# Two stacked cross-attention layers: the work between the two attention loops, done per pair of batches inside the first loop

## The reference

```python
# layer 0: 16 heads of 8
qkv = x @ w_qkv + b_qkv
x = layer_norm(x + mha(q, k, v) @ w_so + b_so, ln_g, ln_b)
ca = mha(x @ w_q + b_q, y @ w_k + b_k, y @ w_v + b_v) @ w_co + b_co
x = layer_norm(x + ca, ln_g, ln_b)
h = relu(relu(x @ w1 + b1) @ w2 + b2)          # 128 -> 512 -> 512
x = layer_norm(x + h @ w3 + b3, ln_g, ln_b)
# layer 1: 16 heads of 64
h = layer_norm(x, gamma, beta)
attn = softmax((h @ Wq) . (context @ Wk)) * 64 ** -0.5
x = x + (attn . (context @ Wv)) @ Wo + bo
```

## Time and profile before

| what | us |
|---|---|
| median of 3 runs | 1124.32 (1124.01 to 1125.93) |
| the profiled execution's own time | 1120.81 |
| its span, first to last instruction | 1119.0 |
| PE busy | 1036.5 (93%) |
| PE loading weights | 737.2 (66%) |
| DVE busy | 756.5 (68%) |
| ACT busy | 570.2 (51%) |
| POOL busy | 390.0 (35%) |
| mean granted clock of PE | 0.960 |

### The profile page before, as it was taken

How to read it: one execution, slowest core, us unless ns; L and a number is a source line. 1 busy time by engine, 2 the same in 40 slices (tenths; PEclk the granted TensorE clock), 3 DMA queues, 4 the chain that set the end, 5 groups by cost and what they waited for, 6 DMA issues and landing times. The chain is left out here.

```text
span 1119.0 us, 31601 instructions
## 1 busy us (share of the span) xinstructions
PE 1036.5 (93%) x12044; PEld 737.2 (66%) x12044; DVE 756.5 (68%) x1406; ACT 570.2 (51%) x1135; POOL 390.0 (35%) x273
## 2 busy tenths in 40 slices
PE   5975899999999998979697999999999999999997
PEld 2551576666666665655534777777777777777786
DVE  4646778887788878520685676767767677767652
ACT  2531577776777765742244444444444444444442
POOL 4823111111211123020103554555545455545542
PEclk9886899999999999989798999999999999999998
DMA  3503533444434443030002111111111111111100
GB/s 98 140 2 104 145 118 124 132 138 143 132 121 124 148 141 89 2 98 1 1 23 72 46 48 56 39 37 56 53 56 50 38 53 31 45 53 56 35 3 4
DMA packets 47021, 79.90 MB, mean 71 GB/s; under 512 B 6978, under 2 KB 33812, under 8 KB 46964
## 3 DMA queue, kind: packets, MB, share of 16 engines
q1 hardware_dynamic: 46964, 79.10, 23.6%
HBM read 50.93 MB, written 21.96 MB: 65 GB/s over the span
## 5 line engine op out<-in xcount | busy, mean ns | idle before, releaser
L1362 ACT ACTIVATE P<-PS 125x448 f32<-125x448 f32 x384 | 207.1, 544 | 270.0 <-PE PS L1271 268.0
L1252 POOL TENSOR_TENSOR Pl<-P 125x896 f16<-125x896 f32 x128 | 229.9, 1801 | 241.9 <-ACT P L1362 241.9
L1000 DVE TENSOR_REDUCE m<-PS 128x1 f32<-128x500 f32 x336 | 220.7, 674 | 119.8 <-PE PS L991 118.0
L906 DVE TENSOR_REDUCE m_part<-PS 128x1 f32<-128x500 f32 x336 | 212.4, 674 | 64.1 <-PE PS L809 62.9
L884 ACT ACTIVATE Pb<-PS 125x448 f32<-125x448 f32 x384 | 187.9, 544 | 36.2 <-PE PS L784 34.8
L1287 PE MATMUL PS<-cNh,P 125*128 125x97 f16 x1344 | 197.9, 208 | 0.1
L1289 PE MATMUL PS<-cNh,Pl 125*128 125x97 f16 x1344 | 197.4, 207 | 0.0
L1288 PE MATMUL PS<-cNl,P 125*128 125x96 f16 x1344 | 196.8, 206 | 0.0
L1288 PEld LDWEIGHTS PS<-cNl,P 125*128 125x128 bf16 x1344 | 131.8, 98 | 25.4
L1287 PEld LDWEIGHTS PS<-cNh,P 125*128 125x128 bf16 x1344 | 131.2, 98 | 15.8 <-issue 3.2
L809 PE MATMUL PS<-KH,Qmx 128*128 128x500 f16 x336 | 129.6, 388 | 11.9 <-PEq L682 8.2
(11 more groups left out here) (167 smaller groups left out, 1531.2 us busy)
## 6 DMA issues: line engine op xcount, KB each, us to landing
Kst<-k_halves SPq DMA_DIRECT2D x144, 125.0 KB, 2.7
k_halves<-KH SPq DMA_DIRECT2D x16, 750.0 KB, 3.3
cx<-in_ctx SPq DMA_DIRECT2D x16, 562.5 KB
d_cx<-in_ctx SPq DMA_DIRECT2D x16, 562.5 KB
c_halves<-cHi SPq DMA_DIRECT2D x16, 281.2 KB, 2.6
c_halves<-cLo SPq DMA_DIRECT2D x16, 281.2 KB, 3.2
cTh<-c_halves SPq DMA_DIRECT2D x16, 281.2 KB, 3.0
cTl<-c_halves SPq DMA_DIRECT2D x16, 281.2 KB, 3.9
```

Source lines behind the costliest of these rows:

```text
L906: nc.vector.tensor_reduce(m_part[:, t, part:part + 1], PS[:, 6 + k % 2, 0:SP], AX.X, ALU.max).then_inc(s_reduced, 1)
L1000: nc.vector.tensor_reduce(m21[:, t, part:part + 1], PS[:, S1[k % 2], 0:SP], AX.X, ALU.max).then_inc(n_red, 1)
L1252: nc.gpsimd.tensor_tensor(Pl[:, c % NP], P1[:, c % NP], high, ALU.subtract).then_inc(n_low_p, 1)
L1362: nc.scalar.activation(P1[:, c % NP, half * HALF:(half + 1) * HALF], PS[0:KC, u % 3, 0:HALF], ACT.Exp).then_inc(n_exp, 1)
```

## The change

The stage in the middle is left only for the last pair of batches. For the pairs t = 0 to 6 its work is done within the loop of the first cross attention, in the bodies of the pair after it (`mid`, t = i - 1), in matmuls of 112 columns into one bank, FB = 2, which the scores give up (SBANKS is 2 where they had 3). The square root is worked out on DVE by three Newton steps. The weights' transposes and products go to the opening, beside the maximum pieces of batch 0; the tile Wvo now lies in Pb's memory. The absorbed queries go to DRAM (`qk_halves`) and are loaded from there. Cut to its core:

```diff
+        def absorb(pe, t, r):
+            if r == 0: pe.wait_ge(f_kept, t * 2 + 2)
+            elif r == 1: pe.wait_ge(att_kept, ...)
+            else: pe.wait_ge(g_low, t * 4 + r - 1)
+            for k in range(4):
+                mm = pe.matmul(PS[0:DC, G_BANKS[r], k * TP:(k + 1) * TP], Wqk[:, 4 * r + k, :], Tm[:], start=True, stop=True)
+        def spread_of(dve, at, src):
+            dve.wait_ge(f_link, at)
+            nc.vector.bn_stats(st6[:], src).then_inc(f_link, 1)
+            dve.wait_ge(f_link, at + 1)
+            nc.vector.memset(passed[:], 0.0)
+            nc.vector.bn_aggr(mv[:], st6[:]).then_inc(f_link, 1)
+            dve.wait_ge(f_link, at + 2)
+            nc.vector.tensor_scalar(half_var[:], mv[:, 1:2], EPS, -0.5, ALU.add, ALU.mult).then_inc(f_link, 1)
+            dve.wait_ge(f_link, at + 3)
+            nc.vector.tensor_scalar(root[:].bitcast(I32), half_var[:].bitcast(I32), -0.5, ROOT_GUESS, ALU.mult, ALU.add).then_inc(f_link, 1)
+            for n in range(ROOT_STEPS):
+                dve.wait_ge(f_link, at + 4 + 2 * n)
+                nc.vector.tensor_scalar(grown[:], root[:], root[:, 0:1], half_var[:, 0:1], ALU.mult, ALU.mult).then_inc(f_link, 1)
+                dve.wait_ge(f_link, at + 5 + 2 * n)
+                nc.vector.tensor_scalar(root[:], grown[:], 1.5, root[:, 0:1], ALU.add, ALU.mult).then_inc(f_link, 1)
+            dve.wait_ge(f_link, at + SPREAD)
+        def norm_cross(dve, t):      # add, spread_of, normalise into nm
+        def norm_hidden(dve, t):     # add, spread_of, gain and bias into Xm
+        def norm_twice(dve, t):      # spread_of(Xm), normalise into nm
...
 first cross attention, SP
+                    if par == 1 and not (isinstance(i, int) and i < 1):
+                        store_queries(sp, i - 1)       # waits g_low t * 4 + 4, two DMAs
 POOL
                         wait_for(pool, st_done, b * NC * 2)
+                        wait_for(pool, m_laid, b + 1)
...
+                    if isinstance(i, int) and b == 0:
+                        norm_to_residual(pool, x_steps, R_CO)
+                    if isinstance(i, int) and b == -1:
+                        pool.wait_ge(wvo_kept, 4)
+                        nc.gpsimd.tensor_tensor(Wvo16[:, 1], Wvo, Wvo16[:, 0], ALU.subtract).then_inc(wvo_split, 1)
+                    if par == 1 and not (isinstance(i, int) and i < 1):
+                        residual(pool, i - 1)
+                        move_residual(pool, i - 1)
 PE
                 turn_context, k == 0:
+                if par == 0 and mode == LOOP:
+                    wait_for(pe, g_low, (i - 1) * 4)
                 scores_t:
+                        if isinstance(i, int) and n == 0:
+                            pe.wait_ge(wvo_kept, 4)
-                        wait_for(pe, exp_done, n * 2 * NC + u - 2)
+                        wait_for(pe, exp_done, n * 2 * NC + u - 1)
                 body, step c:
+                        if mid and par == 1 and c < 4:
+                            hidden_2(pe, t, c)         # before the step's second piece
                         for k in pieces[1:]:
                             score_piece(i, par, k)
+                        if at_start and c < 3:
+                            turn_weights(pe, c)
+                        if at_start and c in (6, 9):
+                            multiply_weights(pe, (c - 6) // 3)
+                        if mid and par == 0:           # c == 9: out_project, 12: turn_pair(0), 13: hidden_1
+                        if mid and par == 1:           # c == 5: hidden_3, 9: turn_pair(1), c >= 10: absorb(c - 10)
 ACT
+                    if isinstance(i, int) and b == 0:
+                        act.wait_ge(wvo_split, 1)
+                        # even: c == 12 keep_pair(0), 13 keep_hidden(0)
+                        # odd: c == 4 keep_hidden(1), 9 keep_pair(1), c >= 10 queries_high(c - 10)
 DVE
+                        if mid and par == 1:
+                            if c == 6:
+                                norm_hidden(dve, t)
+                            if c == 8:
+                                norm_twice(dve, t)
                         for k in pieces[1:]:
                             reduce_piece(i, par, k)
...
                         nc.vector.tensor_tensor(mneg[:, QT:], mhigh[:], mtop[:], ALU.subtract).then_inc(m_ready, 1)
+                        if mid and par == 0:
+                            norm_cross(dve, t)
+                        if mid and par == 1:
+                            queries_low(dve, t, 0)
                         dve.wait_ge(m_turned, n + 1)
...
+                    if mid and par == 1:
+                        for r in range(1, 4):
+                            queries_low(dve, t, r)
 stage in the middle
-                (all of it)
+                SP: load_halves of batch 0, d_cx, load_halves of batch 1, store_queries(NT - 1)
+                PE, ACT, DVE, POOL: the same steps for t = NT - 1, one after the other,
+                PE: out_project, pieces 0-3, turn_pair(0), piece 4, hidden_1, pieces 5-7, hidden_2,
+                    pieces 8-9, hidden_3, pieces 10-16, turn_pair(1), piece 17, absorb(0..3) with pieces 18-20
+                DVE: norm_cross, reductions 0-9, norm_hidden, norm_twice, reductions 10-17, queries_low(0..3) with 18-20
```

More of the change, by code:

```diff
@@ L89, in spread, with over_pairs @@
     return ap.unsqueeze(dim).broadcast_to(shape[:dim] + [n] + shape[dim:])
-def over_pairs(eng, body, before=(), last=1):
+def over_pairs(eng, body, before=(), last=1, first=1):
     for i, par in before:
         body(i, par)
-    for par in (0, 1):
-        body(0, par)
-    with eng.Fori(1, NT - last) as i:
+    for i in range(first):
+        body(i, 0)
+        body(i, 1)
+    with eng.Fori(first, NT - last) as i:
         body(i, 0)
@@ new lines, in hidden_2, with hidden_3 @@
+        def hidden_2(pe, t, m):
+            if m == 0:
+                pe.wait_ge(f1_kept, t + 1)
+            for k in range(4):
+                mm = pe.matmul(PS[:, FB, m * TP:(m + 1) * TP], w2s[:, k, m * 128:(m + 1) * 128], hid1[:, k, :], start=(k == 0), stop=(k == 3))
+            if m == 3:
+                mm.then_inc(f2, 1)
+        def hidden_3(pe, t):
+            pe.wait_ge(f2_kept, t + 1)
+            for k in range(4):
+                mm = pe.matmul(PS[0:TP, FB, 0:D], hid2[:, k, :], w3s[:, k, :], start=(k == 0), stop=(k == 3))
+            mm.then_inc(f3, 1)
@@ new lines, in move_residual, with store_queries @@
+        def move_residual(pool, t):
+            pool.wait_ge(f_normed, t * 2 + 2)
+            pool.wait_ge(table_in, 16)
+            nc.gpsimd.tensor_copy(X[:, bass.ds(t, 1), :], Xm[:].unsqueeze(1)).then_inc(x_moved, 1)
+        def store_queries(sp, t):
+            sp.wait_ge(g_low, t * 4 + 4)
+            for half in range(2):
+                sp.dma_start(qk_halves[bass.ds(t * 2, 2), half].rearrange("b p n -> p b n"),
+                             QKs[:, half].rearrange("p j h q -> p j (h q)")).then_inc(qk_out, 16)
@@ new lines, in pieces @@
+                def pieces(at, n):
+                    for k in range(at, at + n):
+                        score_piece1(pe, -1, 1, k)
+                out_project(pe, t)
+                pieces(0, 4)
+                turn_pair(pe, t, 0)
+                pieces(4, 1)
+                hidden_1(pe, t)
+                pieces(5, 3)
+                for m in range(4):
+                    hidden_2(pe, t, m)
+                pieces(8, 2)
+                hidden_3(pe, t)
+                pieces(10, 7)
@@ L1179, in program, with pieces @@
-        ffn.close()
+                t = NT - 1
+                def pieces(at, n):
+                    for k in range(at, at + n):
+                        reduce_piece1(dve, -1, 1, k)
+                norm_cross(dve, t)
+                pieces(0, 10)
+                norm_hidden(dve, t)
+                norm_twice(dve, t)
+                pieces(10, 8)
+                for r in range(4):
+                    queries_low(dve, t, r)
+                    if r < 3:
+                        pieces(18 + r, 1)
```

405 lines of the change are left out of this document (233 added, 172 removed).

## The result

The changed kernel takes 1172.3 us (median of 4 runs, 1168.9 to 1175.1) against 1124.2 before (4 runs, 1123.3 to 1125.9): a ratio of 1.0425, 95% interval 1.0394 to 1.0456, or 48 us more. Forecast were 1158 within 1122 to 1186, so sign and range held and the size was 14 us short.

A forecast was written before the change was run, and what follows sets the result against it. TensorE was taken to bound both cross-attention loops. Against the profiled 1120.8 us the terms -109 + 34 - 2.9 + 62 + 39 + 5 + 9 - 8 + 5 gave +34: 1155, on the median 1158, range 1122 to 1186.

The forecast's parts named there:

- Steps 1 to 3: Middle stage goes, -109.0; last pair's chain stays there, +34; second loop's entry no longer waits for queries, -2.9.
- step 2: Middle stage: the last pair's chain stays alone in it, 29 plus 5 for first loads and half clock, +34.
- step 3: Entry to second loop: wait for batch 1's queries goes, -2.9; storing and reloading queries through DRAM costs nothing.
- Step 4: First loop: TensorE's added matmuls and transposes, 8.9 us a pair, all on the path, +62.
- Step 5: First loop: TensorE waits for VectorE's new norm chains at turn_pair(0), late score pieces and turn_context, 5.6 a pair, +39.
- Step 10: First loop: slow-clock stretches after TensorE's new waits, between 0 and 36 us, taken as +5.
- The clock rival: First loop: every wait of about 1.5 us is followed by a slow-clock stretch, 36 for 5: 1189, chance 0.2.
- Step 6: First loop: two score banks for three make scores wait for the exponential before last, 0.3 a batch, +5.
- Step 8: First loop: POOL waiting for m_laid before laying queries ends two long stalls at VectorE's mneg, -8.
- Step 7: Opening: weights' transposes and products among reductions, and Wvo sharing Pb's memory, delay the first exponential, +9.
- The rival that the middle isn't really left: Middle stage: last pair's chain and weights cost as much as before what they hid, 50 for 34: 1174, chance 0.07.
- The faster rival: First loop: VectorE's chains hide beside TensorE's new work, waits and clock under 1.4 us a pair: 1114, chance 0.15.

The follow-up runs named there:

- a_store_late: Changed kernel with SyncE's wait for the last pair's store of queries moved from the middle stage's end into its own stream of the second loop: 1165.9 us.
- b_early_load: Kernel before, with POOL waiting for m_laid before laying queries and batch 1's halves for the second loop loaded a stage earlier: 1106.5 us.
- a_less_hidden2: Changed kernel with twelve of hidden_2's sixteen matmuls a pair left out: 1154.3 us.
- a_two_steps_late: a_store_late with two Newton steps in each root in place of three: 1144.9 us.
- b_two_banks: Kernel before, with two score banks in place of three in the first cross attention: 1115.9 us.
- b_pool_wait: Kernel before, with one line added by which POOL waits for m_laid before it lays the next batch's queries: 1110.4 us.
- a_no_steps: Changed kernel with the three Newton steps of each reciprocal root left out: 1125.6 us.
- a_no_pool_wait: Changed kernel without the line by which POOL waits for m_laid before it lays queries: 1181.3 us.

## Why the prediction was right, and where it was short

- **Steps 1 to 3, the middle.** Forecast -75 to the second loop's first score, measured -65.1. The chain from the out-projection to the last subtraction took 38.9 (607.22 to 646.08) where 29 + 5 was forecast. The norms and pieces took about what was said (6.91 for the last two norms), and the loads of the first queries took some 3 of the 5. At a mean clock of 0.61 the three hidden layers took 11.6 for 7.8 (615.28 to 626.9) and the absorbs 7.8 for 6.5; this is the part of step 2 that was too small. The step that failed is the sentence in step 3, "Cost nothing; if that cover went, turn_context would wait". It looked at SyncE inside the loop only. The last pair's store ends the stage, where no engine has anything else: 4.49 us, of which a_store_late brought back 3.2. The entry itself: -2.9 forecast, -4.6 in the second loop, -3.9 in b_early_load.
- **Step 4, TensorE's work.** On the path, though not "all of it": 70 to 80% by a_less_hidden2. 9.8 us a pair in place of 8.9: a float32 matmul of 112 columns takes 0.25 in the hidden layers and 0.21 in the absorbs, its switch of operands included, where 0.757/4 = 0.19 came from one of 448. Mis-sized by 6 us.
- **Step 5, waits.** Places and order held, and so did the lengths: 1.55 at turn_pair(0) (forecast 1.5), 2.27 + 0.59 at the pieces (3.5), 0.68 at turn_context (0.7). But the half clock behind the wait at the pieces, 3.4 us and so 1.7 a pair, stands for waits as well, as the two pairs of a_two_steps_late show. Taken together VectorE's lag at the pieces is some 4.5, not 3.5, and step 5 comes to 6.8 a pair in place of 5.6, 8 us in all.
- **Step 10, clock.** The +5 was about right: a stretch that has a price of its own came in three of six pairs, 1.0 to 1.2 us each, 3 to 4 in all. The clock rival (36) was wrong for the reason that stood against it.
- **Step 6** had +5: by b_two_banks against b_pool_wait 0.4 a pair, some 3.
- **Step 8** had -8, and the wait brought 13.5 in the kernel before and 9 in the one after. Without it the change would have lost more. It had left out the short stall of every pair, 0.4 us, which stands in its own.
- **Step 7** had +9 and got +11.6 in the profiled execution, +5 to +10 in the eight others with the same opening. The chain was the one that it named; it came out above 9 in this execution, whose clock there was 0.72.
- Together for the loop, an estimate from these parts: 69 for TensorE's work, 48 for step 5, 4 for the clock, 3 for the bank, less some 12 of stalls, is 112 where the table has +110 and 103 was forecast. TensorE's work is counted in full here, so the sum is good to some us only. The 18 us by which the sum was short are 7 there, 10 in the middle and 3 in the opening, less 2 in the second loop. On the medians it was 14, in part because the profiled execution of the kernel before lay 3.4 us under its median. That errors of both signs met so near the forecast is partly luck.
- The rival that the middle isn't really left (50 in place of 34) came nearer than its chance of 0.07: 46.1 to the first score, in which 2.6 of entry, the same as before, were not in the 34. The 46.1 also lies outside the 30 to 40 between the loops that was named as a sign, and a pair at 62.6 to 63.8 is above its 60.
- The faster rival needed waits and clock under 1.4 us a pair; they measured 5 to 8. The range was said to take in the clock rival, but ended at 1186, below that rival's 1189, and the faster rival's 1114 lay below its lower end. Neither mattered to the result.

Could the idea pay? With all Newton steps gone, TensorE's work (7 x 9.8 = 69) and the opening (12) still stand against 65 + 5 saved in the middle and at the entry. That agrees with the 1125.6 of a_no_steps, POOL's wait included, 19 behind the kernel before with the two edits of b_early_load.

## What to carry to other kernels

Work moved from an idle-looking stage into a loop that its engine bounds is paid at nearly full price (70 to 80% here), and each short dependent chain beside it is paid in waits of the bounding engine; before such a move, add up what lies between the chain's input and its reader on the engine that runs it. Look first for single stalls in the profile (one operation of 0.17 us that took 4.40): here one wait on the engine that shares the port was worth 1.2% and the whole restructuring -4.3%. A trailing wait for a store, where all engines meet, is on everyone's path (VectorE stood 4.49 us). And price a small edit by a stretch of the loop, not by the total alone, and against a kernel that has the same stalls in that stretch: two banks for three seemed free against the kernel before and cost 0.4 us a pair against b_pool_wait.

## What the hardware showed that was not expected

- **Code.** 22 small matmuls a pair, with next to no work, cost 50 us (a_more_code, 1222.3 against 1172.3), in two loops of which the second's body was unchanged. The instruction queue moved 127 packets of 16.4 KB in place of 45, and TensorE stood some 3 to 5 us at nine turns of the loops. A turn of the kernel after has 734 matmul records on TensorE and as many weight loads in the first loop, 1468, and the second about 6025 x 2 / 8 = 1506; waits and branches are not in these counts, and a float32 matmul leaves two records, so the number of instructions isn't known from them. The Trainium skill (Runtime: NRT & Kernel Launch, Instruction fetch mechanics) says that code comes in blocks of 16 KiB and that a branch to code no longer held makes the engine wait for a fetch; the packets' size and the place of the stalls agree. It gives TensorE room for 2048 instructions; no run here shows that number, and the records of both bodies lie below it. Seven added float32 matmuls, 14 records, were enough too (109 packets). How few would be was not tried.
- **The shared port is not closed to everything.** While POOL ran its row of operations, norm_cross's Newton links on 112x1 kept their 0.27 and 0.21 us (a_no_pool_wait, 323.02 to 324.65, as without), and the 112x128 operation behind them went from 0.35 to 0.89. In the earlier trace rows it was a 128x7 operation that stood for 4.40 us, until POOL's four operations and the one behind them (442.02 to 444.35) were done. The tensor_tensor on 128x7 at 231.83 took 0.55 and ended inside POOL's first four, 231.79 to 233.90. Why these differ was not tried.
- **The clock after waits of one length.** In the kernel after, waits of 1.55 to 1.57 us at the same instruction (L843) were followed by some 3.4 us at granted clock 0.50 in three of six bodies (260.47 is one) and by none in three (387.83 is one); waits of 0.96 to 1.01 were followed by none in six (a_two_steps_late). Of six waits of 1.71 in that run, at a piece, four had such a stretch behind them and two had none (396.36 is one).
